# A graph layer on one core: the query row of a tile is copied into a PSUM bank by ScalarE, and VectorE's product reads it there

## The reference, cut to what matters

```
qe = q[:, c, :]                      # query of the edge's target node
ke = k[:, r, :]; ve = v[:, r, :]     # key and value of its source node
sim = einsum('hed,hed->eh', qe, ke) * scale
m = segment_max(sim, c); p = exp(sim - m[c]); s = segment_sum(p, c)
agg = segment_sum((p / s[c]).T[..., None] * ve, c)
```

## Time and profile before

| | |
|---|---|
| median of three runs | 3283.86 us (3280.67 to 3298.52) |
| span of the profiled execution | 3389.2 us |
| edge loop, first to last product (L1365) in the trace | 337.7 to 2808.2 us |
| VectorE busy over the span | 2436.3 us (72%) |
| POOL busy over the span | 2440.7 us (72%) |
| TensorE busy over the span | 2255.9 us (67%) |
| ScalarE busy over the span | 960.6 us (28%) |

### The profile page before, as it was taken

The page is one execution under the profiler, slowest core; times in us unless marked ns, Lnnn a source line. Parts: engine busy times, 40 slices in busy tenths (PEclk is TensorE's granted clock), DMA queues, the critical chain, the costliest instruction groups (busy, mean ns, idle before and its releaser), DMA issues. The chain is left out here.

```text
span 3389.2 us, 38967 instructions
## 1 busy us (share of the span) xinstructions
PE 2255.9 (67%) x9400; PEld 1778.9 (52%) x9401; DVE 2436.3 (72%) x3389; ACT 960.6 (28%) x4083; POOL 2440.7 (72%) x2220
## 2 busy tenths in 40 slices
PE   5681476767666676757787777455555552579998
PEld 4570364545455554645555445334344441569998
DVE  4672586877686786878888767777788883546665
ACT  2220354645445463510011000000000001335543
POOL 4447687777777787877777777777777775548776
PEclk8895687878788787878778778777778775579999
DMA  5745666666666666677777776666666654723341
GB/s 192 253 146 147 172 181 189 180 183 184 184 186 179 186 182 184 182 202 214 211 217 222 216 206 194 182 182 185 184 182 180 182 165 146 239 80 77 88 90 25
DMA packets 258308, 591.12 MB, mean 174 GB/s; under 512 B 49410, under 2 KB 135505, under 8 KB 257565
## 3 DMA queue, kind: packets, MB, share of 16 engines
q0 software_dynamic: 150480, 467.10, 50.5%
q1 hardware_dynamic: 97947, 109.47, 9.8%
q10 hardware_dynamic: 9296, 9.44, 0.8%
HBM read 519.05 MB, written 71.76 MB: 174 GB/s over the span
## 5 line engine op out<-in xcount | busy, mean ns | idle before, releaser
L971 POOL DMA_INDIRECT wide<-kv_d,arena x1099 | 1279.8, 1164 | 379.0 <-issue 347.4
L1265 PE MATMUL ps<-wide,arena 128*128 128x264 f32 x2432 | 785.0, 480 | 401.6 <-issue 253.0
L1265 PEld LDWEIGHTS ps<-wide,arena 128*128 128x128 f32 x2432 | 570.5, 240 | 603.4 <-issue 324.8
L971 POOL DMA_INDIRECT arena<-kv_d,arena x539 | 610.6, 1133 | 184.6 <-issue 168.0
L1368 DVE TENSOR_REDUCE arena<-arena 128x64 f32<-128x2048 f32 x229 | 523.5, 2286 | 7.9
L1265 PE MATMUL ps<-arena 128*128 128x264 f32 x1216 | 374.5, 463 | 170.6 <-issue 110.4
L1365 DVE TENSOR_TENSOR arena<-wide 128x2048 f32<-128x2048 f32 x153 | 350.9, 2293 | 166.0 <-DMA wide<-kv_d,arena 151.6
L1401 DVE TENSOR_TENSOR wide<-wide,ps 128x2112 f32<-128x2112 f32 x152 | 357.1, 2349 | 139.4 <-issue 65.5
L1265 PEld LDWEIGHTS ps<-arena 128*128 128x128 f32 x1216 | 271.8, 229 | 270.7 <-issue 148.5
L135 PE MATMUL ps<-halves 128*128 128x256 f32 (+2 forms) x2304 | 361.9, 319 | 3.3 <-DVE halves L1634 1.6
L135 PEld LDWEIGHTS ps<-halves 128*128 128x128 f32 x2304 | 331.4, 192 | 31.2 <-POOL halves L1644 3.6
(11 more groups left out here) (312 smaller groups left out, 3090.3 us busy)
## 6 DMA issues: line engine op xcount, KB each, us to landing
wide<-kv_d,arena POOLq DMA_INDIRECT x1099
arena<-in_w SPq DMA_DIRECT2D x16, 1024.0 KB
kv_d<-wide SPq DMA_DIRECT2D x49, 260.0 KB
arena<-xn_d SPq DMA_DIRECT2D x98, 128.0 KB
arena<-kv_d,arena POOLq DMA_INDIRECT x539
hb_d<-arena SPq DMA_DIRECT2D x16, 516.0 KB
q_d<-wide SPq DMA_DIRECT2D x49, 128.0 KB
xn_d<-arena SPq DMA_DIRECT2D x7, 896.0 KB
```

The costliest lines, as they stand in the source:

```text
L971: e.indirect_dma_start(out=kvb[k][:, j, :], out_offset=None, in_=kv_d, in_offset=bass.IndirectOffsetOnAxis(ap=ixb[k][:, j:j + 1], axis=0)) ...
L1265: m = e.matmul(psE[(k + 1) % 3][:, 0:264], ident, kvb[b][:, j, 256:ROW], start=(j == 0), stop=(j == J - 1))
```

## The change

ScalarE gets an operation `query()`: one activation (copy) of the 256 floats of a tile's query row from `qsf` in SBUF to `q_ps`, half of a PSUM bank (`ps[2]`) that the loop did not use. It runs once before the loop, and then in each body, between the copy of the row numbers and the wait for `e_d`: if the tile of the next step is another one, `query()`; else an empty instruction. Both raise a new semaphore, `e_q`. To know the tile, ScalarE loads one more register in each body. VectorE's `scores` now waits for `e_q` (and issues an empty instruction) before it waits for the rows, and reads the query row in PSUM; it no longer needs the register with the tile's place, so it loads three values in place of four and computes no address.

```
+        q_ps = ps[2][:, 0:256]
...
+            def query():
+                e.activation(q_ps, qsf[:, bass.ds(val(e, qa, NT * BLK) * 5, 256)], ACT.Copy).then_inc(e_q, 1)
+
+            query()
...
+                e.reg_mov(qb, qa)
+                e.load([qa], tabF[:, bass.ds(at * 4 + 3, 1)])
                 e.load([t6, w6, p6], tabF[:, bass.ds(at * 4 + 4 * RING - 1, 3)])
                 e.wait_ge(e_prod, g_)
                 e.activation(ixb[k], ixf[...], ACT.Copy).then_inc(e_ix, 1)
+                with e.If_ne(qa, qb):
+                    query()
+                with e.Else():
+                    e.nop().then_inc(e_q, 1)
                 e.wait_ge(e_d, g_)
...
-            def scores(k, count, arrived, q_row):
+            def scores(k, count, arrived):
+                q_row = q_ps
+                e.wait_ge(e_q, count)
+                e.nop().then_inc(e_dm, 1)
                 e.wait_ge(e_arr[k], arrived)
                 e.tensor_tensor(prod.rearrange("p (j n) -> p j n", n=256), kvb[k][:, :, 0:256],
                                 q_row.unsqueeze(1).to_broadcast([128, J, 256]), ALU.mult).then_inc(e_prod, 1)
...
-                e.load([ar, p, w_, q_at], tabF[:, bass.ds(val(e, cg, CH - 14) * 4, 4)])
+                e.load([ar, p, w_], tabF[:, bass.ds(val(e, cg, CH - 14) * 4, 3)])
...
-                scores((k + 1) % RING, cn, ar, qsf[:, bass.ds(val(e, q_at, NT * BLK) * 5, 256)])
+                scores((k + 1) % RING, cn, ar)
```

More of the change, by code:

```diff
@@ L846, in gps_layer_kernel @@
         e_x, e_bs = [[esem(f"{n}{i}") for i in range(RING)] for n in ("x", "bs")]
-        e_xs, e_ix, e_i0, e_go = [esem(n) for n in ("xs", "ix", "i0", "go")]
+        e_xs, e_ix, e_i0, e_go, e_q = [esem(n) for n in ("xs", "ix", "i0", "go", "q")]
         e_bp, e_bc, e_br = [esem(n) for n in ("bp", "bc", "br")]
@@ L1013, in _ @@
         def _(e):
-            g_, tf, ns, sd, p6, w_, w1_, w2_, w3_, w4_, o_at, fc, tp, u, bc, bd = regs(
-                e, "a_", ["g", "tf", "ns", "sd", "p6", "w", "w1", "w2", "w3", "w4", "o_at", "fc", "tp", "u", "bc", "bd"],
-                [0, 0, 0, 0, 0, 0, 0, 0, 0, 0, 0, 1, 0, 0, 0, 1])
+            g_, tf, ns, sd, p6, w_, w1_, w2_, w3_, w4_, o_at, fc, tp, u, bc, bd, qa, qb = regs(
+                e, "a_", ["g", "tf", "ns", "sd", "p6", "w", "w1", "w2", "w3", "w4", "o_at", "fc", "tp", "u", "bc", "bd", "qa", "qb"],
+                [0, 0, 0, 0, 0, 0, 0, 0, 0, 0, 0, 1, 0, 0, 0, 1, 0, 0])
             e.nop().then_inc(e_ao, 1)
@@ L1284, in _ @@
         def _(e):
-            cg, cn, c6, more, ar, p, w_, q_at, w1_, w2_, tf, tq, qf, ns, so, sa_, sl = regs(
-                e, "v_", ["g", "cn", "c6", "more", "ar", "p", "w", "q_at", "w1", "w2", "tf", "tq", "qf", "ns", "so", "sa", "sl"],
-                [0, 1, RING - 3, 0, 0, 0, 0, 0, 0, 0, 0, 0, 0, 0, 0, 0, 0])
+            cg, cn, c6, more, ar, p, w_, w1_, w2_, tf, tq, qf, ns, so, sa_, sl = regs(
+                e, "v_", ["g", "cn", "c6", "more", "ar", "p", "w", "w1", "w2", "tf", "tq", "qf", "ns", "so", "sa", "sl"],
+                [0, 1, RING - 3, 0, 0, 0, 0, 0, 0, 0, 0, 0, 0, 0, 0, 0])
             e.wait_ge(sv.h, sv.n)
@@ L1368, in scores @@
                 e.tensor_reduce(S_ps[:, 0:8 * J], prod.rearrange("p (n d) -> p n d", d=32), AX.X, ALU.add).then_inc(e_red, 1)
-            scores(0, 1, 16 * J, qsf[:, 0:256])
+            scores(0, 1, 16 * J)
             def step():
```

## The result

The changed kernel takes 3019.69 us (median of 4 runs, 3014.33 to 3027.99), the kernel before 3287.26 us beside it (4 runs): ratio 0.918, 95% interval 0.916 to 0.921, or 268 us less. Forecast were 3222 us and a range down to 3120. The direction was right, the size four times too small, and the time lies outside the range.

The account below looks back on a forecast made before the run. The prediction took POOL as nearly saturated, with VectorE's 166 us of waits for rows as the limit of the gain. Its terms, -151 - 2 + 73 + 18 = -62 us, took 3284 to 3222 us, range 3120 to 3325 us.

Parts of the forecast that it names:

- Whatever POOL gains, VectorE can take back only the 166 us: Edge loop: VectorE's product waits 166 us for fetched rows; that, not POOL's 318 us, was to measure the gain.
- the first term: VectorE's waits for rows before the product: 166 us fall to 15 us, a net gain of 151 us.
- The fetches: POOL's fetches beside the product: no longer held up, 316 us freed, 0.96 us each.
- The product's own time: VectorE's product with one PSUM input: 2282 ns, 8 to 11 ns less, -2 us in all.
- The new wait: VectorE's product waiting for ScalarE's query copy: +73 us, from 16 runs of late steps; bounds 0 and 182.
- ScalarE's instructions: ScalarE's extra register load, compare with branch, and copy or empty instruction per body: +18 us, bounds 0 and 33.
- POOL does not wait: ScalarE's refill of `ixb` comes before the new piece, so POOL was not to wait for it.
- VectorE's queue: One wait and one empty instruction more, one address computation less at each product: taken as 0, bounds -13 and +13 us.
- Rival A: The new wait of the product for ScalarE costs next to nothing: -174 us, 3110 us; chance 0.16.
- Rival B: ScalarE becomes the bound through the new wait, in the loop's first half: +64 us, 3348 us; chance 0.15.
- Rival D: No measurable change: same terms, with waits for ScalarE of 120 to 150 us, 3267 to 3300 us; chance 0.20.
- Rival C: The PSUM input doesn't free POOL; fetches under the product stay at 2 to 3 us: 3330 us; chance 0.04.

Follow-up runs that it names:

- late kind: Comparisons in which the kernel before takes 3369 to 3372 us; what makes the kind is open.
- quick kind: Comparisons in which the kernel before takes 3284 to 3289 us; the times of before and after are of this kind.
- e5_before: Control: the kernel before with two small neutral edits, run again on the quick kind; 3289.46 us, ratio 1.0001.
- e1_sbuf: The changed kernel, but with the query row copied into SBUF instead of PSUM, on the late kind; 3392.96 us, ratio 1.0074 to before.
- e6_sbuf: Repeat on the late kind of the changed kernel with the query row copied into SBUF; 3398.31 us, ratio 1.0072 to before.
- e7_sbuf: The changed kernel with the query row copied into SBUF, on the quick kind; 3313.77 us, ratio 1.0078 to before.
- e0_before: Control: the kernel before with two small neutral edits, run on the late kind; 3370.08 us, ratio 1.0006.
- e5_flat_after: The changed kernel with the hardware loops of its first 156 steps written out, on the quick kind; 2991.32 us, ratio 0.9099 to before.
- half dose: The changed kernel with both copies made and every second product reading the SBUF one; ratio 0.9532 to before (quick kind), 1.0114 and 1.0129 (late kind).
- e0_after: The changed kernel with two small neutral edits, run again on the late kind; 3407.53 us, ratio 1.0123 to before.

## Why the prediction was wrong, step by step

- **The step that failed: "Whatever POOL gains, VectorE can take back only the 166 us".** It took the idle times of one profiled execution for those of the runs whose median was being forecast, though that execution was 105 us longer than their median. The prediction noted the 105 us and added the difference at the end. It should have asked what the 105 us were. They are the waits of the late kind: 223 us before ScalarE's `take_raw` and 198 us before VectorE's value product, which on the quick kind are 9.6 us (ScalarE's groups of `e5_before`, last fence of this section) and 25 us. Without them the waits for rows are 301 us instead of 166, and the first term measures -275 us in place of -151. Against it stand 32 us more of pauses before L1397 and L1416; that they were hidden before because the rows were late anyway is a reading.
- **The fetches** (316 us free, 0.96 us each): right. Busy time falls from 1890.4 to 1571.7 us, on the quick kind from 1876.4 us, by 305. The measure of the gain was this number less POOL's new waits, 305 - 38 = 267 us, and the text had ruled it out with "not the 318".
- **The product's own time**: right, 2282 ns forecast, 2280 measured; 229 x 12 ns = -3 us.
- **The new wait (+73) and ScalarE's instructions (+18)**: mis-sized on the quick kind, by all of it. The product waits for ScalarE once, 5.4 us. The 49 late steps of the earlier trace rows were of the late kind: counted in the same way, `e5_before` has one. On the late kind the wait has a price: after is 39 us slower than before, the kernel with VectorE's copies, which doesn't wait for ScalarE, 15 and 12 us, so some 25 us are an estimate of it. `e1_sbuf` and `e6_sbuf`, 24 and 26 us slower, don't show it, since `e7_sbuf` is 27 us slower on the quick kind, where the product waits for ScalarE once; in `e1_sbuf` the fetches alone are busy 24 us longer than in `e0_before` (1917.9 against 1894.4 us). "POOL does not wait" for `ixb` was wrong by 11 us.
- **VectorE's queue at 0**: right where the copy is in PSUM, but the shift that the extra instruction makes is worth 29 us where it is not.
- **Rival A** (3110 us, the wait costs nothing) had the mechanism of the quick kind and the same wrong limit. **Rival B** (slower, ScalarE late) came near on the late kind: +64 forecast, +39 measured, and a first stretch of 1122 us against 1076 us in `e0_before`. But its wait is not what eats the gain there: with VectorE's copies and no such wait the fetches are freed too, and there is none either. **Rival D** (no change that can be measured) came on neither kind. **Rival C** is excluded: no fetch beside the product is over 1.05 us, of 386.
- **Of the signs named**: the fetches' mean, the row waits under 40 us, 2280 ns and POOL's waits for buffers came; the 250 us of idle time before the product did not (it came only on the late kind), and the loop of 2140.6 us was the sign given for A.

The Trainium skill, "SBUF — State Buffer", section "Who interferes with whom", recalls a `tensor_tensor` that did not stall a DMA. The rows say otherwise for an indirect DMA on POOL, which reads its row numbers from SBUF: 225 of 288 fetches beside the product were held in `e5_before`, and 0 of 386 in after. "Runtime: NRT & Kernel Launch", a page of the Trainium skill, section "Instruction fetch mechanics", says that a taken branch out of the window stalls for a fetch. The trace agrees as far as it goes: 37 pauses of up to 3.2 us before the total fall to 11 with the jumps written out. VectorE's waits in after, then in `e5_flat_after`:

```profile
DVE arena L1397 <- issue: 100.7, 37, 3.2
```

```profile
DVE arena L1402 <- issue: 30.4, 11, 3.1
```

`take_raw` in `e5_before`, to set beside L1069 in the earlier trace rows:

```profile
L1070 ACT ACTIVATE arena<-ps 128x512 f32<-128x512 f32 x98 | 57.1, 583 | 9.6 <-issue 8.8
```

## What to carry to other kernels

When the profiled execution is some per cent longer than the median that is to be forecast, find out what the difference is made of before any idle time in it is used as a limit; here it was another kind of comparison, on which the same change gave +39 us in place of -268. Where a profile holds far fewer semaphore updates than another of the same program, don't read its "issue" as a wait for nothing. Where one engine is saturated by work that is stretched by another, the gain is the stretch less that engine's new waits, and a sum over its own line (busy and idle) checks it. Before experiments are compared, see that before takes its known time beside them.

## What the runs showed that I had not expected

- The two kinds of comparison: 2.5% apart for before, 13% for after. On the late kind TensorE and ScalarE get their instructions one by one, 0.71, 1.42 or 2.13 us apart, in stretches in which POOL fetches without a pause, and in the two places shown they recover some 3 us after it stops. (POOL fetches with hardly a pause on the quick kind too.) The last stretch of the loop takes 704 to 708 us there in every kernel that I compared (before and after, copy in SBUF, half dose, VectorE's copy, flattened), against 703 us for before and 633.5 us for after on the quick kind. That the fetches starve the instruction supply is an inference from the timing; it was not tried (a shorter lead of POOL where before is late would), and one number speaks against slow loads of code: the DMA packets of the instruction queue take 0.47 us on the mean in the loop of `e0_before` and 0.45 us in `e5_before`. What differs stays open, and with it why the late traces have lost over half of the semaphore updates.
- The data of a fetch arrive as fast on both kinds, so the fetches of the late kind are not short of bandwidth: the last DMA packet of a fetch's rows ends 2.68 us after the fetch's end in `e0_before` and 2.67 us in `e5_before`, 2.71 us in `e0_after` and 2.73 us in after (medians).
- A held fetch ends 0.83 us after the product's end, in all 225 cases of `e5_before` within 0.01 us, and it is one fetch a product. So what two SBUF inputs cost here depends on the phase as well as on the product's length: an instruction that shifts the product by 0.13 us costs 29 us.
